# Decoder layer on one core: another hand-written order of work for the full turns

## The reference, cut to what matters

```
x = _layernorm(x + attn(x))            # 16 query heads, 8 key/value groups, head size 64, causal mask
x = _layernorm(x + xattn(x, ctx))      # 8 heads, 77 context rows, each query sees at most 5 chosen ones
x = _layernorm(x + ffn(x))             # down(silu(gate(x)) * up(x)), 768 hidden, integer weights

q = einsum('bsd,dhe->bshe', x, W_Q); k, v likewise with 8 groups
probs = softmax(where(causal, q.k / 8, -1e6)); z = probs.v; out = z.W_out + b_out
h = silu(gate) * up; return einsum('bsh,dh->bsd', h, wd)
```

## Time and profile before

| | |
|---|---|
| median of 3 runs | 2031.87 us (2030.08 to 2032.34) |
| profiled execution | 2031.16 us, span 2029.4 us |
| PE, PEld | busy 99% and 91% of the span |
| DVE, ACT, POOL | busy 76%, 65%, 19% |
| granted TensorE clock | 0.996 on the mean |
| chain that ended last | PE 97%, DVE 1%, ACT 1%, issue 1% |
| HBM traffic | 29.56 MB read, 8.39 MB written, 19 GB/s |

### The profile page before, as it was taken

The page is one execution under the profiler, slowest core; times in us unless marked ns, Lnnn a source line. Parts: engine busy times, 40 slices in busy tenths (PEclk is TensorE's granted clock), DMA queues, the critical chain, the costliest instruction groups (busy, mean ns, idle before and its releaser), DMA issues.

```text
span 2029.4 us, 50598 instructions
## 1 busy us (share of the span) xinstructions
PE 2000.8 (99%) x18176; PEld 1837.8 (91%) x18176; DVE 1545.9 (76%) x5708; ACT 1324.1 (65%) x3992; POOL 377.6 (19%) x624
## 2 busy tenths in 40 slices
PE   8999999999999999999999999999999999999987
PEld 7899999999999999999999999999999999999886
DVE  6877777777777777777777777777777777777764
ACT  8866666667666666666666666666666666666642
POOL 3112111211211111112121112112121211121121
PEclk9999999999999999999999999999999999999998
DMA  5100000000000000000000000000000000000000
GB/s 164 32 8 22 19 21 12 11 19 19 22 12 19 11 19 22 19 12 22 8 21 19 12 22 8 22 19 22 12 19 11 19 22 19 12 11 19 13 7 11
DMA packets 49606, 41.19 MB, mean 20 GB/s; under 512 B 19536, under 2 KB 47568, under 8 KB 49360
## 3 DMA queue, kind: packets, MB, share of 16 engines
q1 hardware_dynamic: 49360, 37.96, 6.4%
HBM read 29.56 MB, written 8.39 MB: 19 GB/s over the span
## 4 chain that ended last, share of the span: by engine, by line
PE 97%; DVE 1%; ACT 1%; issue 1%; SPq 0%; DMA 0%; POOL 0%; POOLq 0%; DVEq 0%; ACTq 0%
PE gen L442 20%; PE gen L443 19%; PE gen L444 19%; PE s_ps L582 9%; PE z_ps L624 7%; PE gen L530 3%; PE pt_ps L603 3%; PE gen L543 3%; PE gen L539 3%; PE pt_ps L604 3%; PE pt_ps L608 3%; PE z_ps L626 3%; PE gen L510 2%; PE gen L501 1%; PE gen L554 1%
## 5 line engine op out<-in xcount | busy, mean ns | idle before, releaser
L955 ACT ACTIVATE SM<-SM,least 128x128 f32<-128x128 f32 (+1 forms) x1024 | 452.4, 447 | 35.1 <-DVE least L1480 35.0
L885 ACT ACTIVATE PT<-pt_ps 128x512 f32<-128x512 f32 (+1 forms) x512 | 237.8, 486 | 237.6 <-PE pt_ps L604 235.4
L1480 DVE CUSTOM_DVE_ANT_0 SM<-s_ps,causal 128x128 f32<-128x128 f32 (+1 forms) x1024 | 314.6, 352 | 19.6 <-PE s_ps L582 14.7
L1493 DVE TENSOR_SCALAR SM<-SM,total 128x128 f32<-128x128 f32 (+1 forms) x1024 | 282.7, 339 | 9.1
L1859 POOL TENSOR_TENSOR H_lo<-gated,H_hi 128x256 fp32r<-128x256 f32 x192 | 143.2, 752 | 513.0 <-ACT H_hi L885 513.0
L582 PE MATMUL s_ps<-KT,QT 64*128 64x128 f32 (+1 forms) x2048 | 201.5, 335 | 1.4 <-ACT KT L885 0.7
L938 ACT ACTIVATE gated<-gen 128x256 f32<-128x256 f32 x192 | 73.8, 385 | 197.6 <-PE gen L444 197.5
L955 ACT ACTIVATION_READ_ACCUMULATOR SM<-SM,least 128x1 f32 x1024 | 197.0, 192 | 0.0
L1457 DVE SCALAR_TENSOR_TENSOR gated<-gated,gen 128x256 f32<-128x256 f32 x192 | 80.9, 421 | 115.8 <-ACT gated L938 115.4
L624 PE MATMUL z_ps<-PT,Vt 128*64 128x256 f32 x1024 | 168.1, 399 | 0.0
L582 PEld LDWEIGHTS s_ps<-KT,QT 64*128 64x128 f32 x2048 | 147.6, 187 | 21.8 <-issue 6.4
(11 more groups left out here) (185 smaller groups left out, 6504.7 us busy)
## 6 DMA issues: line engine op xcount, KB each, us to landing
xT_in<-in_xT SPq DMA_DIRECT2D x32, 256.0 KB, 2.9
x_in<-in_x SPq DMA_DIRECT2D x32, 256.0 KB, 2.8
out<-rows SPq DMA_DIRECT2D x32, 256.0 KB, 2.2
ctx_in<-in_ctxT SPq DMA_DIRECT2D x32, 77.0 KB, 2.8
mask_in<-in_maskT SPq DMA_DIRECT2D x32, 77.0 KB, 2.6
SX<-in_wq SPq DMA_DIRECT2D x1, 512.0 KB, 6.4
rows<-in_wv SPq DMA_DIRECT2D x1, 512.0 KB, 7.2
xwk<-in_xwkv SPq DMA_DIRECT2D x1, 512.0 KB, 7.9
```

The costliest lines, as they stand in the source:

```text
L885: return act.activation(o, i, ACT.Copy)
L955: ins = act.activation(part, part, ACT.Exp, scale=-1.0, bias=least[:, i % 4, n:n + 1], accum_out=total[:, i % 4, n:n + 1])
L1480: ins = dve.tensor_tensor_reduce(SM[:, i % 4, at:at + keys], s_ps[bank][:, col:col + keys], causal[:, S - keys:S], -SCALE, -3 * NEG, ALU.a ...
L1493: ins = dve.tensor_scalar(part, part, total[:, i % 4, n:n + 1], None, ALU.mult)
```

## The change

Only the order of calls in the full turns changes, on all four computing engines, and ITEMS with it. No instruction is added or removed in a turn; the first and last turns and SyncE stay as they are. Of TensorE's queue:

- Turn start: aQ1 and XOUT follow transposed(6); then transposed(7), aK1, the context keys aXK, scores(1), the values 6 and 7, T3, and aQ2 on its own before transposed(0). Before, aXK and XOUT came first, then transposed(6), a run aK1, aQ1, aQ2, transposed(7), T3, values, scores(1).
- FFN3 stands between aV1 and aV0 instead of behind them.
- values(1) follows values(0); FFN4 and aQ3 are one run; XQ0 and XQ1 are one run ahead of transposed(3), and SIM10 comes right behind that.
- FFN5 moves from behind aQ3 to the front of the run nQ0, nK0, DOWN1, DOWN0.

The lists of ACT, DVE and POOL are put in an order that fits. ACT takes exps(6,1) before the copy of XPV0, and split_context from the turn's start to behind split_x; POOL's context_low moves behind gated_low(4). Of ACT's and DVE's lists the later part of the turn is shown here.

```diff
--- before.py
+++ after.py
@@ -30,8 +30,8 @@
     (1, "oT201"), (1, "oT210"), (1, "oT211"), (1, "oXPV0"), (1, "oXPV1"),
 ]
 ITEMS = [
-    "aXK", "fXOUT", "aK1", "aQ1", "aQ2", "fT3", "fFFN0", "oOUT0", "oOUT1", "fFFN1", "fFFN2", "aV1", "aV0",
-    "fFFN3", "oT10", "oT11", "fFFN4", "aQ3", "fFFN5", "oXQ1", "oXQ0", "oSIM10", "oSIM11", "oSIM00", "oSIM01",
+    "aQ1", "fXOUT", "aK1", "aXK", "fT3", "aQ2", "fFFN0", "oOUT0", "oOUT1", "fFFN1", "fFFN2", "aV1", "fFFN3",
+    "aV0", "oT10", "oT11", "fFFN4", "aQ3", "oXQ0", "oXQ1", "oSIM10", "oSIM11", "oSIM00", "oSIM01", "fFFN5",
     "nQ0", "nK0", "fDOWN1", "fDOWN0", "oT201", "oXV", "oT200", "oT211", "oT210", "oXPV0", "oXPV1",
 ]
 LAST_ITEMS = [
@@ -716,17 +716,17 @@
 
             def turn_between(t):
                 t.scores(0)
+                t.transposed("o", 6)
+                t.fill("aQ1")
+                t.fill("fXOUT")
+                t.transposed("o", 7)
+                t.fill("aK1")
                 t.fill("aXK")
-                t.fill("fXOUT")
-                t.transposed("o", 6)
-                t.fill("aK1")
-                t.fill("aQ1")
-                t.fill("aQ2")
-                t.transposed("o", 7)
-                t.fill("fT3")
+                t.scores(1)
                 t.values("o", 6)
                 t.values("o", 7)
-                t.scores(1)
+                t.fill("fT3")
+                t.fill("aQ2")
                 t.transposed("a", 0)
                 t.fill("fFFN0")
                 t.fill("oOUT0")
@@ -735,25 +735,25 @@
                 t.fill("fFFN2")
                 t.transposed("a", 1)
                 t.fill("aV1")
+                t.fill("fFFN3")
                 t.fill("aV0")
-                t.fill("fFFN3")
                 t.scores(2)
                 t.fill("oT10")
                 t.fill("oT11")
                 t.values("a", 0)
+                t.values("a", 1)
                 t.fill("fFFN4")
+                t.fill("aQ3")
                 t.transposed("a", 2)
-                t.fill("aQ3")
-                t.fill("fFFN5")
+                t.fill("oXQ0")
                 t.fill("oXQ1")
                 t.transposed("a", 3)
-                t.fill("oXQ0")
-                t.values("a", 1)
                 t.fill("oSIM10")
                 t.scores(3)
                 t.fill("oSIM00")
                 t.values("a", 2)
                 t.values("a", 3)
+                t.fill("fFFN5")
                 t.fill("nQ0")
                 t.fill("nK0")
                 t.fill("fDOWN1")
@@ -1123,79 +1123,79 @@
...
+                t.split_x()
+                t.split_context()
                 t.probs_out("a", 3, 0)
                 t.probs_out("a", 3, 1)
+                t.gated_high(3)
+                t.gated_high(4)
+                t.fill("fFFN5")
                 t.gated_high(5)
-                t.split_x()
-                t.exps(6, 0)
                 t.fill("nQ0")
                 t.context_exps(0)
                 t.fill("nK0")
+                t.exps(6, 0)
                 t.context_exps(1)
+                t.z_high_out("a", 1)
                 t.probs_out("a", 4, 0)
-                t.z_high_out("a", 1)
+                t.probs_out("a", 4, 1)
                 t.fill("oT201")
-                t.probs_out("a", 4, 1)
                 t.fill("oXV")
                 t.fill("oT200")
-                t.fill("oT211")
                 t.probs_out("a", 5, 0)
                 t.probs_out("a", 5, 1)
+                t.fill("oT211")
                 t.fill("oT210")
+                t.exps(6, 1)
                 t.fill("oXPV0")
-                t.exps(6, 1)
+                t.exps(7, 0)
+                t.fill("oXPV1")
                 t.z_high_out("a", 2)
-                t.fill("oXPV1")
-                t.exps(7, 0)
                 t.exps(7, 1)
 
             def last_turns(t, u, v):
@@ -1645,63 +1645,63 @@
...
                 t.probabilities(5)
+                t.z_low_out("a", 0)
                 t.fill("oSIM10")
                 t.fill("oSIM11")
-                t.z_low_out("a", 0)
                 t.masked(6, 0)
+                t.fill("oSIM00")
                 t.fill("oSIM01")
-                t.fill("oSIM00")
                 t.context_shift(0)
+                t.fill("fFFN5")
                 t.context_shift(1)
                 t.context_probs(0)
                 t.fill("fDOWN1")
+                t.masked(6, 1)
                 t.fill("fDOWN0")
                 t.context_probs(1)
                 t.z_low_out("a", 1)
-                t.masked(6, 1)
                 t.masked(7, 0)
+                t.moments_3()
                 t.masked(7, 1)
-                t.moments_3()
+                t.probabilities(6)
                 t.fill("oXPV0")
-                t.probabilities(6)
+                t.y()
                 t.fill("oXPV1")
                 t.z_low_out("a", 2)
-                t.y()
                 t.probabilities(7)
 
             def last_turns(t, u, v):
@@ -1909,13 +1909,13 @@
                 t.x_bias()
                 t.deviation_2()
                 t.gated_low(0)
-                t.context_low()
                 t.both_deviations()
                 t.gated_low(1)
                 t.gated_low(2)
                 t.gated_low(3)
+                t.gated_low(4)
+                t.context_low()
                 t.x_low()
-                t.gated_low(4)
                 t.gated_low(5)
                 t.deviation_3()
```

More of the change, by code:

```diff
@@ L1125, in turn_between @@
             def turn_between(t):
-                t.split_context()
+                t.probs_out("o", 6, 0)
+                t.fill("aQ1")
+                t.probs_out("o", 6, 1)
+                t.exps(0, 0)
+                t.probs_out("o", 7, 0)
+                t.exps(0, 1)
                 t.fill("aXK")
-                t.probs_out("o", 6, 0)
-                t.exps(0, 0)
-                t.probs_out("o", 6, 1)
+                t.probs_out("o", 7, 1)
                 t.fill("aK1")
[L1132 to L1135, removed]
+                t.z_high_out("o", 3)
+                t.fill("fT3")
+                t.exps(1, 0)
                 t.fill("aQ2")
-                t.fill("fT3")
-                t.z_high_out("o", 3)
-                t.exps(1, 0)
                 t.probs_out("a", 0, 0)
+                t.probs_out("a", 0, 1)
                 t.fill("fFFN0")
@@ L1143, in turn_between @@
                 t.exps(2, 0)
-                t.probs_out("a", 0, 1)
                 t.gated_high(0)
+                t.fill("fFFN1")
                 t.exps(2, 1)
-                t.fill("fFFN1")
                 t.fill("fFFN2")
+                t.gated_high(1)
+                t.probs_out("a", 1, 0)
+                t.fill("aV1")
                 t.exps(3, 0)
-                t.gated_high(1)
-                t.fill("aV1")
-                t.probs_out("a", 1, 0)
+                t.fill("fFFN3")
+                t.exps(3, 1)
+                t.probs_out("a", 1, 1)
                 t.gated_high(2)
                 t.fill("aV0")
-                t.fill("fFFN3")
-                t.exps(3, 1)
+                t.fill("oT11")
                 t.fill("oT10")
-                t.probs_out("a", 1, 1)
-                t.fill("oT11")
-                t.gated_high(3)
                 t.nx_high_out()
+                t.exps(4, 0)
                 t.fill("fFFN4")
+                t.exps(4, 1)
+                t.exps(5, 0)
+                t.fill("aQ3")
+                t.exps(5, 1)
                 t.probs_out("a", 2, 0)
[L1164 to L1167, removed]
                 t.probs_out("a", 2, 1)
-                t.exps(5, 0)
-                t.exps(5, 1)
+                t.fill("oXQ0")
                 t.fill("oXQ1")
-                t.fill("oXQ0")
-                t.gated_high(4)
                 t.z_high_out("a", 0)
+                t.split_x()
+                t.split_context()
                 t.probs_out("a", 3, 0)
                 t.probs_out("a", 3, 1)
+                t.gated_high(3)
+                t.gated_high(4)
+                t.fill("fFFN5")
                 t.gated_high(5)
-                t.split_x()
-                t.exps(6, 0)
                 t.fill("nQ0")
@@ L1647, in turn_between @@
                 t.masked(0, 0)
+                t.masked(0, 1)
+                t.masked(1, 0)
                 t.fill("fXOUT")
-                t.masked(0, 1)
+                t.masked(1, 1)
                 t.moments_2()
-                t.masked(1, 0)
+                t.probabilities(0)
                 t.x2()
-                t.masked(1, 1)
-                t.probabilities(0)
+                t.masked(2, 0)
+                t.z_low_out("o", 3)
                 t.fill("fT3")
-                t.z_low_out("o", 3)
                 t.masks()
-                t.masked(2, 0)
                 t.fill("fFFN0")
+                t.probabilities(1)
                 t.masked(2, 1)
                 t.fill("oOUT0")
-                t.probabilities(1)
                 t.masked(3, 0)
@@ L1667, in turn_between @@
```

(7 more changed lines are left out.)

## The result

The changed kernel takes 2044.74 us (median of 4 runs, 2042.95 to 2046.15), the kernel before beside it 2032.11 (4 runs, 2030.08 to 2032.49): ratio 1.0063, interval 1.0052 to 1.0075. The forecast was 2034.6 with a range of 2026 to 2042. The profiled execution took 2043.47, 12.3 more than that of before. One execution of the kernel before, beside the second group of experiments, took 9574.38 us; it is in no ratio.

A forecast was written before the change was run, and what follows sets the result against it. TensorE, busy 2000.8 of 2029.4 us, was taken as the bound. Stretches summed to +0.06 a turn, x 29 = +1.8, and +1.0 once: +2.8, giving 2033.9 profiled and 2034.6 forecast, range 2026 to 2042.

The forecast's parts named there:

- second price: Step of 256-column products inside a TensorE run: 0.1133 or 0.1179 us; runs led by FFN0 and FFN4 always short.
- Start of turn to FFN0: TensorE from turn start to FFN0: 15.17 us before and after, no change, bounds -0.1 and +0.1.
- first price: TensorE's cost of changing array shape: leaving 128 x 128 about 0.09 us, another shape 0.10; entering values 0.05, scores 0.10.
- V1, FFN3, V0: This middle stretch of the turn: same items, same shapes around them, 0.00 us, 0.05 either way.
- FFN4 to SIM: Stretch FFN4 to SIM: 8.05 to 8.08 us, +0.03; lost cover 0.30 eats shape change 0.24 and faster aQ3.
- FFN5 to DOWN0: Last run of the turn: 8.56 to 8.59 us, +0.03; short-step gain 0.28 spent on 0.29 bank wait at nK0.
- Once: First full turn only: TensorE's transposed(6) waits for p_ready, +0.97 us once.
- POOL, SP, DOWN1's low half: Moved context_low and x_low, next context load: no cost; H's low half for DOWN1 fits by 0.12 us.
- Rival (a): Wait makes nK0 the leader, its run falls back to the long step: 0.22 us a turn, 2040.5 to 2041; chance 0.24.
- Rival (c): Other leads turn short (aQ1 with XOUT, aK1, aQ2, XQ0 with XQ1): 0.39 us a turn, 2023; chance 0.08.
- (b): Waits smaller than in the last turns: 2026 without the bank's 0.29, 2017 without SIM's too; chance 0.15.
- (d): A missed wait, above all DOWN1 behind H's low half: each 0.1 a turn is 2.9 us; 2037 to 2046; chance 0.09.

The follow-up runs named there:

- e6: Kernel before with only aQ2 moved, out of its run to stand alone between scores(1) and transposed(0); 2055.17 us, ratio 1.0119 to before.
- e1: Kernel after plus one product of 64 rows and 8 columns ahead of transposed(0), which FFN0 follows; 2048.16 us, ratio 1.0085 to before.
- c1: Kernel after plus an 8-column product with all 128 rows ahead of transposed(0), so the array shape stays; 2050.11 us, ratio 1.0091 to before.
- e2: Kernel after with transposed(0) ahead of aQ2 instead of behind it, so aQ2 leads a run of 96; 2045.26 us, ratio 1.0072 to before.
- e7: Kernel after with values(1) moved from behind values(0) to between transposed(3) and SIM10; 2054.35 us, ratio 1.0115 to before.
- c2: e2 plus the 64-row product of e1, placed between T3 and transposed(0); 2047.26 us, ratio 1.0078 to before.

## Why the prediction was wrong

The step that failed is one that got no line of its own in the sum: FFN0's run, 84 products, taken over unchanged at 9.65. The second price says "those led by FFN0 and FFN4 always short", and I read that as a property of the lead. For FFN0 it was a property of what stood ahead of it: scores and transposes. The change puts aQ2's split products there, and the run goes long: 9.98, which is 9.6 of the 11.3 us. The forecast prices aQ2's new place as an item and never asks what it does to the run behind it. e6 shows that this one move does it; e1, with its control c1, that a change of shape ahead of the transposes undoes it. The other gains and losses nearly cancel.

Point by point:

- *Start of turn to FFN0*, 15.17: came at 15.04 on the mean. The error has the same root. aQ1 with XOUT was taken as long, since aK1 had been, but behind scores and transposes it is short (-0.13). The other items add up, also aQ2's isolated place, 1.49 for 1.50. One of them by luck: the context keys took 1.14 as forecast, but their first start, 0.235 behind scores, costs only 0.136 behind aK1, which the sum left out against its own first price, and the last one, 0.026 ahead of a split run, costs 0.220 ahead of scores, where 0.09 was added.
- *V1, FFN3, V0*: 4.33 for 4.34, right.
- *FFN4 to SIM*: right. SIM10 1.06 behind transposed(3), aQ3 at the short step, 1.36.
- *FFN5 to DOWN0*: the mechanism was right, the size of the wait 0.07 short: 0.36 for 0.29, 2.0 us over the turns. The turns with a long part cost 0.8 us more. The bank came when computed; TensorE started 0.15 behind that read.
- *Once*: 0.93 for 0.97, right.
- *POOL, SP, DOWN1's low half*: no wait, right.
- Rival (a), nK0's run falling back behind the wait: did so in 2 of the 25 turns in which FFN5 and nQ0 were short. It is the rival whose time was nearest (2040.5), for a reason that was hardly there. That it was only 2 is in part luck: in e2, with this part of the turn unchanged, it fell back in 13 of 22.
- Rival (c), other leads turning short: half true. aQ1 with XOUT and aQ2 did; aK1 alone and XQ0's run stayed long. "Their history is all long" was the history of their neighbours.
- Rivals (b) and (d): no wait smaller, none missed.

The page "TensorE: Matmul & The Clock Gate" of the Trainium skill, section Back-to-back issue gap, has one step for a given number of columns. Rows 4 and the runs here disagree: at 256 columns a run has 0.113 or 0.118, at the same granted clock of 1.00.

Open:

- What in TensorE holds the step. The weight loads (PEld) show little: in FFN0's run of before and of after the next load starts 0.001 to 0.005 behind a product's start. The loads of the short one are recorded with 0.187 or 0.188, those of the long one to about a third with 0.192.
- Why T3's group between values and transposes gives the long step.
- Runs with no transposes ahead: FFN4 behind values short in all turns but 6 (of e7, behind a wait), nQ0 mostly long, and XOUT behind the context keys of before mixed. XOUT goes two turns short, two turns long, with one slip, in 29 turns whose orders are all the same. And FFN5's run, with the same items around it, has its later part long in 4 turns of after, in 18 of e1 and e2, in 19 of c2. So the items right ahead do not decide every run. What else does is not known.
- Wide products seem to bring the short step too. V1's products have 512 columns and stand behind a split run and a group of transposes, where 256-column runs were long, yet FFN3 right behind V1 is short in all 29 turns of all kernels here. In after, FFN3 to V0:

```profile
618.49 0.28 PE L442 MATMUL gen<-NT_hi,wg_hi 128*128 128x256 f32 x1
...
619.87 0.39 PE L442 MATMUL gen<-wv_hi,xTs_hi 128*128 128x512 f32 x1
```

12 products in 1.38, 0.113 each once the first two are over. Whether V1 ahead of FFN0 would have kept its run short was not tried; it would need no product that does nothing, as e1's.

## What to carry to other kernels

If one engine is busy all the time, compare the step of equal instructions across runs before pricing an order, and tabulate it by what stands ahead of the run, not by who leads it; then ask it anew for each run whose neighbour changes, also for those that the diff leaves in place. In this kernel it paid to start long runs behind a change of shape and one group of transposes, and to isolate short ones. And before an item is moved, list whose copy it covers: aQ2, values(1) and transposed(4) each covered one or two other chains, and taking them away cost 0.3 to 1.1 us a turn, mostly more than the step is worth.

## What the hardware showed that I had not expected

- Two stable steps for the same products at full granted clock: 8.16 or 8.17 against 8.48 us for 72 products. Each holds for 60 to 96 products without drift, if no wait falls into the run.
- One product of 64 rows and 8 columns ahead of six transposes switches the run behind them from long to short (e1, c2); one of 128 rows does not (c1). It costs 0.46 a turn, more than the 0.35 it brings.
- A wait can change the step in either direction (after: two turns each way).
- The same release costs differently: TensorE started 0.15 behind the read of FFN5's bank at nK0, and 0.05 to 0.06 behind the read of a bank in the last turns of before. What makes the difference is not shown.
